# Joining the attention heads of an even and an odd group on one 128-row operand

## The reference, cut to what matters

```
def _L0_xattn_ref(Q, K, V, mask, Wq_w, Wq_b, Wk_w, Wk_b, Wv_w, Wv_b, Wo_w, Wo_b):
    q = (Q @ Wq_w + Wq_b).reshape(b, tq, H, DK).transpose(0, 2, 1, 3)
    k = (K @ Wk_w + Wk_b).reshape(b, tk, H, DK).transpose(0, 2, 1, 3)
    v = (V @ Wv_w + Wv_b).reshape(b, tk, H, DK).transpose(0, 2, 1, 3)
    scores = einsum('bhqd,bhkd->bhqk', q, k) / sqrt(DK)
    scores = where(mask == 0, -1e9, scores)
    attn = softmax(scores, axis=-1)
    out = einsum('bhqk,bhkd->bhqd', attn, v)
    out = out.transpose(0, 2, 1, 3).reshape(b, tq, c)
    return out @ Wo_w + Wo_b
x = x + xattn(layernorm(x), ctx, ctx, mask, ...)
x = x + ffn(layernorm(x), ...)        # router, top 2 of 8 experts, a shared expert
```

## Time and profile before

| | before |
|---|---|
| median of 3 runs | 950.74 us (946.79 to 951.39) |
| the profiled execution | 948.47 us, span of the trace 946.7 us |
| PE busy | 854.2 us, 90% of the span |
| DVE, ACT, POOL busy | 577.1, 401.7, 384.7 us |
| copies `ps_o` to `o32` (L524), 16 of them | first at 91.8, last at 467.2 us: one iteration takes 25.0 us in the mean |
| last product of the output projection (L834) | 486.8 us |

### The profile page before, as it was taken

How to read it: one execution, slowest core, us unless ns; L and a number is a source line. 1 busy time by engine, 2 the same in 40 slices (tenths; PEclk the granted TensorE clock), 3 DMA queues, 4 the chain that set the end, 5 groups by cost and what they waited for, 6 DMA issues and landing times. The chain is left out here.

```text
span 946.7 us, 22062 instructions
## 1 busy us (share of the span) xinstructions
PE 854.2 (90%) x7868; PEld 528.8 (56%) x7868; DVE 577.1 (61%) x1236; ACT 401.7 (42%) x656; POOL 384.7 (41%) x559
## 2 busy tenths in 40 slices
PE   4669899999999999987826989999999999999998
PEld 3334355545555455533422667777777775666666
DVE  5565577878888887764344744444444443667775
ACT  3124556555655665555413224344344343233231
POOL 6322336577766655556342401111111114455530
PEclk9789999999999999998766999999999999999999
DMA  9343344455544444341215312222222222233521
GB/s 287 99 139 113 108 125 133 129 160 141 152 131 114 132 129 127 107 96 48 83 67 176 104 42 80 85 79 80 82 82 80 80 73 90 84 91 92 183 93 45
DMA packets 96571, 102.72 MB, mean 109 GB/s; under 512 B 16274, under 2 KB 80146, under 8 KB 96468
## 3 DMA queue, kind: packets, MB, share of 16 engines
q1 hardware_dynamic: 77444, 64.99, 23.5%
q0 software_dynamic: 9936, 27.15, 8.7%
q10 hardware_dynamic: 9088, 9.18, 3.3%
HBM read 62.61 MB, written 38.40 MB: 107 GB/s over the span
## 5 line engine op out<-in xcount | busy, mean ns | idle before, releaser
L628 DVE TENSOR_REDUCE mx<-ps_st 128x4 f32<-128x1024 f32 x128 | 155.6, 1215 | 50.2 <-PE ps_st L745 43.0
L516 ACT ACTIVATE p<-ps_st 128x1024 f32<-128x1024 f32 x128 | 131.0, 1024 | 82.8 <-PE ps_st L761 71.2
L1137 POOL DMA_DIRECT2D sorted_out<-ys x71 | 38.5, 543 | 215.5 <-ACT ys L1196 215.5
L1366 DVE TENSOR_TENSOR hf<-ps_u,gs 128x352 f32<-128x352 f32 x71 | 37.2, 525 | 139.5 <-ACT gs L1182 133.7
L1145 POOL DMA_INDIRECT ya<-sorted_out,packed x64 | 65.0, 1016 | 56.7 <-DVE xr L1327 37.9
L963 POOL DMA_INDIRECT expert_rows<-hrow,slot x64 | 66.7, 1042 | 40.4 <-DVE slot L954 23.9
L777 PE MATMUL ps_o<-p,vx 128*17 128x256 f32 x1024 | 72.2, 402 | 7.5 <-ACT p L516 7.5
L724 PE MATMUL ps_st<-mb_q,identb 64*64 64x512 bf16 x256 | 53.7, 416 | 28.0 <-DMA ks<-qk_scratch 17.2
L1479 PE MATMUL ps_g<-fwh,xgT 128*128 x284 | 75.6, 314 | 2.0 <-DVE xgT L1356 2.0
L1479 PE MATMUL ps_u<-fwh,xgT 128*128 x284 | 75.9, 315 | 0.0
L1412 PE MATMUL ps_u<-hT_blk,sw 128*128 128x512 f16 (+1 forms) x288 | 71.3, 384 | 0.8 <-DVE hf L1315 0.8
(11 more groups left out here) (238 smaller groups left out, 2087.2 us busy)
## 6 DMA issues: line engine op xcount, KB each, us to landing
aw<-ffn_dram SPq DMA_DIRECT2D x20, 544.0 KB, 3.8
xg<-expert_rows SPq DMA_DIRECT2D x71, 128.0 KB, 2.0
sorted_out<-ys POOLq DMA_DIRECT2D x71, 128.0 KB, 2.0
qs<-qk_scratch SPq DMA_DIRECT2D x96, 64.0 KB, 2.9
ks<-qk_scratch SPq DMA_DIRECT2D x96, 64.0 KB, 2.7
xr<-x_dram SPq DMA_DIRECT2D x8, 512.0 KB, 8.3
c<-ctx_dram SPq DMA_DIRECT2D x16, 256.0 KB, 2.7
qk_scratch<-qhl SPq DMA_DIRECT2D x16, 256.0 KB
```

Source lines behind the costliest of these rows:

```text
L516: eng.activation(expo[n % 4][:, :, :], ps_st[pair["T", n]][:, :].rearrange("p (h q) -> p h q", h=4), ACT.Exp, scale=SCALE).then_inc(s_e, 1)
L628: eng.tensor_reduce(mx[b % 2][:, qt, :].rearrange("p (h g j) -> p h g j", h=2, g=HG)[:, :, hg, :], ps_st[pair["S", 8 * b + n]][:, :].rearr ...
```

## The change

Heads of an even group keep their place on rows `32j` to `32j+15`. Heads of an odd group are moved to rows `32j+16` to `32j+31`, which were zero. For this `vx` gets, for each pair of groups, 48 columns: 16 of the even head's values, 16 of ones, 16 of the odd head's values; an even group multiplies by the first 17, an odd one by the last 32. After the multiplication by `rb`, the odd group's columns are added onto the even group's, and the sum (`joined`, 2 x 256 columns) is cast, split and projected. `w_o` is packed without the zero rows, so two operands are contracted in place of four. The sums of even and odd groups now stand on different rows, and `rb` is filled for even groups on 16 rows and for odd groups on the 16 rows under them.

```diff
-        WA = 3 * DC * D + HG * D
+        WA = 3 * DC * D + HC * D
-        vx = [t(f"vx{i}", [P, TT, H, DK + 1], FP32) for i in range(3)]
+        vx = [t(f"vx{i}", [P, TT * HC * 4, 3 * DK], FP32) for i in range(3)]
-        onh = t("onh", [P, HG, SEQ], FP16)
-        onl = t("onl", [P, HG, SEQ], FP16)
+        o_of = o32[:, :].rearrange("p (c s t) -> p c s t", c=HC, s=2)
+        joined = o_of[:, :, 0, :]
+        onh = t("onh", [P, HC, SEQ], FP16)
+        onl = t("onl", [P, HC, SEQ], FP16)
...
-                    eng.wait_ge(s_rr, 64 * (b + 1))
+                    eng.wait_ge(s_rr, 128 * (b + 1))
                     eng.wait_ge(s_oc, b + 1)
                     for g in range(HG):
                         cols = slice(g * SEQ, (g + 1) * SEQ)
                         last = eng.tensor_tensor(o32[:, cols], o32[:, cols], rb[:, cols], ALU.mult)
+                    link(last)
+                    for c in range(HC):
+                        last = eng.tensor_tensor(joined[:, c, :], joined[:, c, :], o_of[:, c, 1, :], ALU.add)
                     last.then_inc(s_n, 1)
                     eng.wait_ge(s_onh, b + 1)
-                    for g in range(HG):
-                        last = eng.tensor_tensor(onl[:, g, :], o32[:, g * SEQ:(g + 1) * SEQ], onh[:, g, :], ALU.subtract)
+                    for c in range(HC):
+                        last = eng.tensor_tensor(onl[:, c, :], joined[:, c, :], onh[:, c, :], ALU.subtract)
...
-                            eng.dma_start(den_scratch[b, 0, :].rearrange("(j c) -> j c", j=4),
-                                          o32[DK:P:32, :]).then_inc(s_dw, 16)
+                            for side in range(2):
+                                eng.dma_start(den_scratch[b, 0, :].rearrange("(j c s t) -> j c s t", j=4, c=HC, s=2)[:, :, side, :],
+                                              o_of[DK - DK * side:P:32, :, side, :]).then_inc(s_dw, 16)
                         elif step == 1:
-                            eng.wait_ge(s_dw, 16 * (b + 1))
+                            eng.wait_ge(s_dw, 32 * (b + 1))
...
-                        elif step == 4:
+                        elif step in (4, 5):
                             eng.wait_ge(s_rw, 16 * (b + 1))
                             if b:
                                 eng.wait_ge(s_n, b)
-                            for j in range(4):
-                                row = den_scratch[b, 1:2, j * HG * SEQ:(j + 1) * HG * SEQ]
-                                eng.dma_start(rb[32 * j:32 * j + DK, :], row.broadcast_to([DK, HG * SEQ])).then_inc(s_rr, 16)
+                            for j in (0, 1) if step == 4 else (2, 3):
+                                for side in range(2):
+                                    row = den_scratch[b, 1:2, j * HG * SEQ:(j + 1) * HG * SEQ]
+                                    row = row.rearrange("o (c s t) -> o c s t", c=HC, s=2)[:, :, side, :]
+                                    at = 32 * j + DK * side
+                                    eng.dma_start(rb[at:at + DK, :].rearrange("p (c s t) -> p c s t", c=HC, s=2)[:, :, side, :],
+                                                  row.broadcast_to([DK, HC, SEQ])).then_inc(s_rr, 16)
...
-                            eng.wait_ge(s_rr, 64 * (b + 1))
-                            eng.tensor_tensor(o32[:, :], o32[:, :], rb[:, :], ALU.mult).then_inc(s_n, 1)
+                            eng.wait_ge(s_rr, 128 * (b + 1))
+                            link(eng.tensor_tensor(o32[:, :], o32[:, :], rb[:, :], ALU.mult))
+                            eng.tensor_tensor(joined, joined, o_of[:, :, 1, :], ALU.add).then_inc(s_n, 1)
...
+                c, side = divmod(hg, 2)
+                first, wide = (0, DK + 1) if side == 0 else (DK, 2 * DK)
                 for kt in range(TT):
                     for j in range(4):
-                        last = mm(ps_o[32 * j:32 * j + DK + 1, hg * SEQ:(hg + 1) * SEQ], vx[b % 3][:, kt, 4 * hg + j, :],
+                        last = mm(ps_o[32 * j:32 * j + wide, hg * SEQ:(hg + 1) * SEQ],
+                                  vx[b % 3][:, (kt * HC + c) * 4 + j, first:first + wide],
...
-                                for hg in range(HG):
+                                for c in range(HC):
                                     for wl, xl in TERMS:
                                         w = (awh, awl)[wl]
-                                        last = mm(o, (onh, onl)[xl][:, hg, tt * P:(tt + 1) * P],
-                                                  w[:, WO + hg * D:WO + (hg + 1) * D], start=False,
-                                                  stop=hg == HG - 1 and xl == 1)
+                                        last = mm(o, (onh, onl)[xl][:, c, tt * P:(tt + 1) * P],
+                                                  w[:, WO + c * D:WO + (c + 1) * D], start=False,
+                                                  stop=c == HC - 1 and xl == 1)
...
-    w_o = np.zeros((HG, 4, 32, D), np.float32)
-    w_o[:, :, 0:DK] = a(L0_xattn_Wo_w).reshape(HG, 4, DK, D)
-    w_o = w_o.reshape(HG, P, D).transpose(1, 0, 2).reshape(P, HG * D)
+    w_o = a(L0_xattn_Wo_w).reshape(HC, 2, 4, DK, D).transpose(0, 2, 1, 3, 4)
+    w_o = w_o.reshape(HC, P, D).transpose(1, 0, 2).reshape(P, HC * D)
```

More of the change, by code:

```diff
@@ L25 @@
 HG = 4
+HC = 2
 NE = 8
@@ L305, in _ @@
             eng.wait_ge(s_awl, 1)
-            eng.dma_start(aw32[:, 0:HG * D], w_o).then_inc(s_wo, 16)
+            eng.dma_start(aw32[:, 0:HC * D], w_o).then_inc(s_wo, 16)
             def load_half(j):
@@ L388, in _ @@
             eng.wait_ge(s_wo, 16)
[L389 to L390 removed]
+            link(eng.tensor_copy(awh[:, WO:WA], aw32[:, 0:HC * D]))
+            eng.tensor_tensor(awl[:, WO:WA], aw32[:, 0:HC * D], awh[:, WO:WA], ALU.subtract).then_inc(s_awl, 1)
             def split_half(j):
@@ L500, in _ @@
                                 eng.wait_ge(s_pv, 4 * (b - 2))
-                            for tt in range(TT):
-                                last = eng.activation(vx[b % 3][:, tt, :, 0:DK],
-                                                      bank((kind, b))[:, tt * D:(tt + 1) * D].rearrange("p (h d) -> p h d", h=H),
-                                                      ACT.Copy)
-                                last.then_inc(s_vx, 1)
+                            heads = bank((kind, b))[:, :].rearrange("p (q s j d) -> p q s j d", s=2, j=4, d=DK)
+                            for side in range(2):
+                                at = 2 * DK * side
+                                eng.activation(vx[b % 3][:, :, at:at + DK].rearrange("p (q j) d -> p q j d", j=4),
+                                               heads[:, :, side, :, :], ACT.Copy).then_inc(s_vx, 1)
                             eng.wait_ge(s_vx, 2 * b + 2)
@@ L563, in _ @@
                                 eng.wait_ge(s_o, b)
-                            eng.activation(onh[:, :, :], o32[:, :].rearrange("p (g t) -> p g t", g=HG),
-                                           ACT.Copy).then_inc(s_onh, 1)
+                            eng.activation(onh[:, :, :], joined, ACT.Copy).then_inc(s_onh, 1)
             eng.wait_ge(s_tw, 16 * EARLY)
@@ L704, in _ @@
                         if b >= NB - LATE and step == 6:
-                            eng.wait_ge(s_rr, 64 * (b + 1))
-                            eng.tensor_tensor(o32[:, :], o32[:, :], rb[:, :], ALU.mult).then_inc(s_n, 1)
+                            eng.wait_ge(s_rr, 128 * (b + 1))
+                            link(eng.tensor_tensor(o32[:, :], o32[:, :], rb[:, :], ALU.mult))
+                            eng.tensor_tensor(joined, joined, o_of[:, :, 1, :], ALU.add).then_inc(s_n, 1)
                         if b >= NB - LATE and step == 7:
                             eng.wait_ge(s_onh, b + 1)
-                            eng.tensor_tensor(onl[:, :, :], o32[:, :].rearrange("p (g t) -> p g t", g=HG), onh[:, :, :],
-                                              ALU.subtract).then_inc(s_onl, 1)
+                            eng.tensor_tensor(onl[:, :, :], joined, onh[:, :, :], ALU.subtract).then_inc(s_onl, 1)
                         if step == 2:
```

6 lines of the change are left out of this document (2 added, 4 removed).

## The result

The kernel after the change takes 990.39 us (median of 4 runs, 987.07 to 995.91) against 950.38 us for the kernel before on the same chip: 1.042 times as long, with a 95% interval of 1.038 to 1.047. The forecast was 1008 us with a range of 960 to 1026 us. The sign, the place and the mechanism were right; the size was 17.6 us too large.

The account below looks back on a forecast made before the run. PE was taken to bound the attention stage; a net 3.25 us in each of 14 batches (45.5 us), 12 for clock loss and 2 for the last batches gave 59.5 us onto 948.47: 1008 us, range 960 to 1026.

Parts of the forecast that it names:

- What bounds the kernel: Attention stage: PE sets the pace, busy 25.02 of 25.4 us an iteration, so each microsecond it waits is lost.
- The chain ahead of the cast: DMAs to `rb`, POOL's multiplications and additions, then the cast of `onh`: cast starts 5.45 us later than now.
- the place of the second four DMAs: Step 5 on ACT's queue: first issue at about 340.3, behind unit 1's activations, 3.9 us after the first four.
- the forecast case: Stall at the cast plus clock loss in part of the batches: 990 to 1026 us, chance 0.51.
- From the cast to PE: Eviction of `q` and unit 3's exponential queue behind the cast on ACT; PE's T of unit 4 starts 3.75 us later.
- The second wait of my account: Step 5's issues hold the eviction of `ct`, and through DVE the S of unit 4, 1 to 1.5 us, inside the 3.75.
- What PE saves: Output projection, 14 matmuls in place of 26: 1.31 us a batch, 0.5 counted as gained, bounds 0.3 and 1.31.
- The rest: Batches 14 and 15, divided on DVE: +2 us, bounds -2 and +6; weights, copies and start: 0.
- The wider weights: Values weights of 32 columns cost some 7 ns more a load, 0.2 us a batch, mostly hidden: 0, bound 3 us.
- That the stall is absorbed: Rival: `onh` at most 1.8 us later, T of unit 4 not late, PE's saving shows: 934 us, chance 0.07.
- The kept clock: Rival: same wait before T of unit 4, PE's clock not lowered: 996 us, down to 974; chance 0.24.

Follow-up runs that it names:

- experiment 4: The kernel before with only two of four operands in the output projection (14 matmuls in place of 26, half the heads left out): 945.60 us, ratio 0.995.
- experiment 8: The kernel before with the sums of a batch written by two DMAs in place of one: 954.60 us, ratio 1.005.
- experiment 7: The changed kernel with `rb` filled by four DMAs of 32 rows in step 4 and without the additions: 950.81 us, ratio 1.001.
- experiment 3: The kernel before with its four DMAs to `rb` split over steps 4 and 5, two in each: 955.57 us, ratio 1.005.
- experiment 6: The changed kernel with `rb` filled by four DMAs of 32 rows, all in step 4, additions kept: 959.91 us, ratio 1.011.

## Why the prediction was right, and where it was off

**What bounds the kernel**: right. The loss is PE's, in the attention stage alone.

**The chain ahead of the cast**: right in every link but one. The additions were sized at 1.42 us and take 1.41; the multiplications at 2.85 and take 2.87; the cast at 0.62 and takes 0.63; an issue at 0.53, and the median is 0.44. The term that was mis-sized is the place of the second four DMAs: "3.9 us later than the first four". I had put their first issue behind the start of the last small activation of unit 1. In the iteration shown that activation starts at 344.05, and the first of the second four is issued at 342.77, ahead of the exponential of 343.04. Over the 14 batches the distance is 2.0 to 4.3 us, 2.8 in the mean. ACT's queue issues a DMA while activations ahead of it are still to run; only the order in the queue is kept. POOL so starts 6.87 us behind the first issue in place of my 8.1, and the cast comes 4.1 us later than before in place of 5.45. That is 1.3 us a batch and 19 us over 14 batches, as much as the whole error of 17.6 us. By this error the measured 990.4 us lies at the very edge of the 990 to 1026 us that I gave the forecast case.

**From the cast to PE**: I let 1.70 us of the delay be absorbed (5.45 to 3.75). The table speaks for a soft edge rather than this threshold, though its rows also hold the shorter projection and the clock: with the cast 1.9 us later (four DMAs) a batch already costs 0.85 us, 2.9 us later (no additions) 1.36, 3.45 us later (eight in one step) 2.3, and 4.1 us later (after) 2.9. The slack differs from one iteration to the next, so small delays are charged in part and large ones in full. This fits the additions, which cost PE 3.7 us of idle time in one kernel and 15.0 us in another; no run isolates it. The second wait of my account, the S of unit 4 held up by 1 to 1.5 us through the eviction of `ct`, hardly shows: from 100 to 480 us ACT waited 3.3 us for issue before that eviction, in 5 batches, and PE's waits for DVE's maxima are 11.8 us in all, against 9.3 before. It stood inside the 3.75, so the sum doesn't change.

**What PE saves**: I counted 0.5 of 1.31 us; experiment 4 shows 0.30 (4.8 us over 16 batches), the lower bound, and its profile doesn't show even that between the copies. My reason for not counting all of it, the sums and DVE's order, was a real cost of its own: 4.7 us (experiment 8).

**The rest**: +2 us for the last two batches. From the 15th to the 16th copy it is 20.7 us against 19.2, and behind them nothing was added: +1.5. The wider weights: 0. The loads were heavier than I took them to be:

```profile
L789 PEld LDWEIGHTS ps_o<-p,vx 128*32 128x32 f32 x512 | 15.3, 125 | 23.8 <-issue 12.5 <-ACT p L522 7.7
L789 PEld LDWEIGHTS ps_o<-p,vx 128*17 128x17 f32 x512 | 12.1, 99 | 19.1 <-issue 7.1 <-ACT p L522 6.2
```

That is 26 ns more for 15 columns where I had 7. It is hidden all the same: 16 matmuls with wide weights take 1.07 us, and with narrow ones 1.06. If the effects add up, experiment 7 bounds what it can cost: 950.8 = 950.4 - 4.8 (projection) + 4.7 (sums) + the rest, so the rest is 0.5 us, within an uncertainty of some 4 us.

**Where the 40 us are**, by steps that add up: two steps in place of one 7.7 (990.4 to 982.7), eight DMAs in place of four 22.8 (to 959.9), additions 9.1 (to 950.8), and the rest 0.4, in which the gain of 4.8 and the second DMA of the sums would cancel. The border between the first two is uncertain by some 7 us, their sum of 30.5 is not. The order of the steps matters, as the additions show.

**The rivals.** That the stall is absorbed needed ACT's queue "far ahead of its engine". It does run ahead, by 1.1 us of the 3.9, which is what made the loss smaller, but not far enough. The kept clock (974 to 996) contains the measured time, but the clock was not kept. What that rival got right by number it had wrong by cause.

## What to carry to other kernels

Before a change saves matmuls, count the DMA issues that it adds to a queue with in-order work behind them: here 12 matmuls a batch were worth 4.8 us over the run, one more DMA cost 4.7 us, and four more some 23 us. Merge what a small rearrangement of the data allows to merge (one DMA of 256 KB took 0.63 us to issue, eight of 32 KB 3.5 us), and put the added arithmetic ahead of the transfer that the engine waits for anyway, not behind it. Slack need not be a threshold: where the iterations differ, charge a delay in part from its first microsecond, as with the 5 us of experiment 3.

## What was unexpected of the hardware

- ACT's queue issues DMAs between and ahead of activations that stand before them: at 342.77 us an `rb` DMA is issued 0.27 us before the exponential starts that precedes it in the program, and 1.28 us before the last small activation that does.
- The time of an issue follows the number of DMAs and hardly their size: 0.44 us in the median for 32 KB (128 DMAs) and the same for 64 KB in the kernel before and for 128 KB in experiment 6, 0.63 us for 256 KB with eight rows of DRAM, each repeated over 16 partitions, in one DMA. The Trainium skill ("DMA: Bandwidth & Descriptors", the section on bandwidth) says that transfers under 64 KB are dominated by their descriptors rather than their bytes; here the issuing queue was the cost, with the same preference for fewer and larger ones. No run here measures how long these transfers kept the DMA engines.
- FP32 weights with 32 columns load in 125 ns and with 17 in 99 ns (lines above), and with 128 in 151 ns: not a straight line.
- A multiplication by a value per partition takes POOL 1.6 us for 128x512, more than the addition of two tiles of that size (1.28 us).
